# A four-part graph network on one core: the first gathering in two short-float passes, heavy blocks found from the edge list, the root product first, 16 basis sums inside the counting

## What is computed

```python
def rgcn_gate_layer(x, row, col, edge_type, basis, att, gate_w, root, bias):
    w = jnp.einsum('rb,bio->rio', att, basis)          # 2 x 512 x 512 out of 30 bases
    x_j = x[col]
    for r in range(2):
        gate = jax.nn.sigmoid(x_j @ gate_w[r, :, 0])
        msgs.append(gate[:, None] * x_j @ w[r])
    msg = jnp.where((edge_type == 0)[:, None], msgs[0], msgs[1])
    agg = jax.ops.segment_sum(msg, row, num_segments=x.shape[0])
    return agg + x @ root + bias
h = relu(rgcn_gate_layer(x, row, col, edge_type, basis1, ...))
out = rgcn_gate_layer(h, row, col, edge_type, basis2, ...)
```

## Time and profile before

| | us |
|---|---|
| median of 3 runs (lowest, highest) | 1159.91 (1156.43, 1161.30) |
| the profiled execution | 1161.15 |
| its span | 1159.4 |

### The profile page before, as it was taken

How to read it: one execution, slowest core, us unless ns; L and a number is a source line. 1 busy time by engine, 2 the same in 40 slices (tenths; PEclk the granted TensorE clock), 3 DMA queues, 4 the chain that set the end, 5 groups by cost and what they waited for, 6 DMA issues and landing times. The chain is left out here.

```text
span 1159.4 us, 15448 instructions
## 1 busy us (share of the span) xinstructions
PE 1086.1 (94%) x4410; PEld 607.0 (52%) x4442; DVE 835.8 (72%) x1852; ACT 558.3 (48%) x978; POOL 559.3 (48%) x518
## 2 busy tenths in 40 slices
PE   3989888899999989899999999999999999999997
PEld 1564222344557453655565565555555557446664
DVE  5694677769755153688788788788888867849997
ACT  0221321310332221477777777777777744116663
POOL 1960112233433330667876666666666300027774
PEclk9988989999999999899999999999999999999999
DMA  7995997657211005595554454445454010026665
GB/s 283 341 404 212 360 400 264 231 184 233 84 48 46 13 14 194 132 259 111 114 110 92 101 98 95 100 95 97 98 98 88 1 55 23 9 93 197 203 206 173
DMA packets 60182, 172.66 MB, mean 149 GB/s; under 512 B 12645, under 2 KB 13189, under 8 KB 52552
## 3 DMA queue, kind: packets, MB, share of 16 engines
q0 software_dynamic: 31536, 72.01, 26.6%
q1 hardware_dynamic: 28568, 99.66, 23.4%
HBM read 159.65 MB, written 11.98 MB: 148 GB/s over the span
## 5 line engine op out<-in xcount | busy, mean ns | idle before, releaser
L1664 PE MATMUL PS<-wide,hidT 128*128 128x512 f32 x672 | 302.1, 592 | 2.2 <-DVE hidT L1540 0.4
L705 POOL DMA_INDIRECT rec_scratch<-rec_src,slot_row x84 | 102.5, 1220 | 252.8 <-DMA rec_scratch<-rec_src,slot_row 208.2
L1664 PEld LDWEIGHTS PS<-wide,hidT 128*128 128x128 f32 x672 | 128.6, 191 | 122.8 <-issue 120.5
L1482 POOL DMA_INDIRECT pair_sum<-table_j,counts_rec x84 | 136.7, 1627 | 27.3 <-issue 25.3
L1598 ACT ACTIVATE wide<-PS 128x512 f32<-128x512 f32 x168 | 100.5, 598 | 99.6 <-PE PS L1648 63.5
L1801 POOL DMA_INDIRECT u_space<-table_j,wide x87 | 86.1, 990 | 108.7 <-DMA table_j<-agg_space 81.8
L1474 POOL DMA_INDIRECT pair_sum<-table_i,counts_rec x84 | 89.5, 1066 | 98.9 <-PE PS L1648 59.5
L1603 ACT ACTIVATE wide<-wide,two 128x512 f32<-128x512 f32 x168 | 120.9, 720 | 6.2 <-DVE wide L1533 6.2
L1533 DVE SCALAR_TENSOR_TENSOR wide<-wide 128x512 f32<-128x512 f32 x168 | 116.4, 693 | 5.8
L1491 POOL DMA_INDIRECT rec_scratch<-rec_src,slot_row x84 | 89.5, 1066 | 40.9 <-issue 21.6
L1608 ACT ACTIVATE wide<-wide 128x512 f32<-128x512 f32 x168 | 105.8, 630 | 5.3
(11 more groups left out here) (325 smaller groups left out, 1884.9 us busy)
## 6 DMA issues: line engine op xcount, KB each, us to landing
pieces<-basis_rows SPq DMA_DIRECT2D x56, 1024.0 KB, 7.5
ring<-basis_low SPq DMA_DIRECT2D x30, 256.0 KB, 6.4
w_scratch<-pieces SPq DMA_DIRECT2D x112, 32.0 KB
counts_rec<-rec_scratch SPq DMA_DIRECT2D x1, 2856.0 KB, 9.8
rec_scratch<-rec_src,slot_row POOLq DMA_INDIRECT x168, 2.3
root<-L_gnn_root SPq DMA_DIRECT2D x2, 1024.0 KB, 8.0
rows_in<-in_rows_in SPq DMA_DIRECT2D x2, 1024.0 KB, 13.9
w_rel<-w_scratch SPq DMA_DIRECT2D x1, 2048.0 KB, 11.6
```

Source lines behind the costliest of these rows:

```text
L705: nc.gpsimd.indirect_dma_start(out=rec3_dram, out_offset=bass.IndirectOffsetOnAxis(ap=slot_row[:, 1, t:t + 1], axis=0), in_=rec, in_offset ...
L1482: nc.gpsimd.indirect_dma_start(out=pair_sum[:, t % GOT3, :], out_offset=None, in_=tables[0][1], in_offset=bass.IndirectOffsetOnAxis(ap=idx ...
L1664: m = nc.tensor.matmul(o, hidT[:, t % 2, k * P:(k + 1) * P], w2[:, k, :], start=False, stop=(k == KT - 1), skip_group_check=True)
```

## The change

- **Heavy blocks from the edge list.** `largest`, `mark_heavy` and `heavy` go. Instead VectorE copies the group masks in the sort (`both_kinds` at e = 10), TensorE sums edges per pair of source and target chunk in seven products (`pair_sums`, e = 20), VectorE and TensorE reduce them (`sums_of_groups` at e = 44, `block_sums` at e = 50, `sums_of_blocks` at e = 74), and `heavy_blocks(0)` and `heavy_blocks(1)` follow at e = 74, each six steps longer than before. A block with 4095 or more edges in all counts as heavy.
- **First gathering in short float.** Its ten rows stand in ten slots of their own in `pieces` (`first_rows`); ScalarE rounds them (`first_high`, into the space of `packed`, so behind the last unpacking) and rounds the counts (`counts_rounded`) between the last products, VectorE takes the rests (`first_low`). The two splits of count blocks stand ahead of this, right behind the last unpacking. TensorE takes the first term of all chunks, then waits for all parts, adds the rests and takes the 95 other passes.
- **Order of layer 2.** The five root products stand ahead of the gates and products. SP's program is as before.
- **Basis sums.** 16 of 60 stand in the counting, one behind the one-hots of each tile from 62 to 77; 4, 6, 6, 6, 6 ahead of the chunks' adds, 16 behind them.
- **Records** are set at e = 40 of the sort.
- TensorE loads four block numbers to registers right behind the counting and two more ahead of the second gathering.

```diff
-            rests = pieces_short[:, 4 * NT, :].rearrange("p (j n) -> p j n", j=4)
+            first_hi = nc.alloc_sbuf_tensor_at("first_hi", [P, 2 * NT, D], F32R, offset=packed_at)
+            rests = nc.alloc_sbuf_tensor_at("rests", [P, 4, P], F32R, offset=packed_at + 8 * NT * D)
...
+            FIRST_SLOT = 4 * (RING1 - 1)
+            first_rows = pieces[:, FIRST_SLOT:FIRST_SLOT + 2 * NT, :]
+            first_lo = pieces_short[:, FIRST_SLOT:FIRST_SLOT + 2 * NT, :]
+            first_at = lambda r, c: (2 * c + r + KT) % (2 * NT)
...
-            SUM2_BEFORE_H1 = (16, 11, 11, 11, 11)
+            SUM2_COUNT = range(62, 78)
+            SUM2_BEFORE_H1 = (4, 6, 6, 6, 6)
+            PAIR_SUMS_AT, BLOCK_SUMS_AT = 20, 50
...
+                FIRST_TERMS = [(m_, r, part) for m_ in range(NT) for r in range(2) for part in (first_hi, first_lo)]
+                def gathered_first(c, terms):
+                    for m_, r, part in terms:
+                        pe.wait_ge(sem("counts_short"), 2 * m_ + r + 1)
+                        pe.wait_ge(sem("first_lo" if part is first_lo else "first_hi"), 2 * m_ + r + 1)
+                        m = nc.tensor.matmul(PS[:, c, :], counts_short[r][:, m_, c * P:(c + 1) * P], part[:, first_at(r, m_), :],
...
+                def pair_sums():
+                    pe.wait_ge(sem("src_group"), 3)
+                    for g in range(ET // SUM_TILES):
...
+                pe.wait_ge(sem("heavy_at"), 2)
+                rest_chunk = [rest_numbers(j, 8, NT - 1) for j in range(2)]
+                rest_first = [rest_numbers(j, 12, 2 * NT - 1) for j in range(2)]
                 early_late = Y0_LATE[0]
...
-                for c in range(NT):
-                    gathered_first(c)
+                pe.wait_ge(sem("rests"), 2)
+                for c in range(NT):
+                    gathered_first(c, FIRST_TERMS[:1])
+                pe.wait_ge(sem("first_hi"), 2 * NT)
+                pe.wait_ge(sem("first_lo"), 2 * NT)
+                for j in range(2):
+                    rest(rests[:, j, :], rest_chunk[j], (first_hi, first_lo), rest_first[j])
+                for c in range(NT):
+                    gathered_first(c, FIRST_TERMS[1:]).then_inc(sem("o0_mm"), 1)
                     if c:
                         pe.wait_ge(sem("h1"), c)
                         turn_rows(c - 1, turn(("T1", c - 1), alone))
 
                 for c in range(NT):
-                    if c == 1:
-                        pe.wait_ge(sem("h1"), NT)
-                        turn_rows(NT - 1, turn(("T1", NT - 1), alone))
-                    pe.wait_ge(sem("side_ev"), side["T1", c] + 1)
+                    if c == 0:
+                        pe.wait_ge(sem("root_in"), 32)
+                        for d in range(NT):
+                            if d == 1:
+                                pe.wait_ge(sem("h1"), NT)
+                                turn_rows(NT - 1, turn(("T1", NT - 1), alone))
+                            pe.wait_ge(sem("side_ev"), side["T1", d] + 1)
+                            root_rows(d)
                     gates(1, (c,), turn(("G1", c), alone))
...
-                    if c in HEAVY_AT:
-                        heavy(HEAVY_AT.index(c))
-                pe.wait_ge(sem("root_in"), 32)
-                for c in range(NT):
-                    root_rows(c)
...
                 for j in range(2):
-                    rest(rests[:, j, :], rest_numbers(j, 8, NT - 1), (y_hi, y_lo), rest_numbers(j, 4, 2 * NT - 1))
+                    rest(rests[:, j, :], rest_chunk[j], (y_hi, y_lo), rest_numbers(j, 4, 2 * NT - 1))
...
+                    if e == 10:
+                        both_kinds()
+                    if e == 40:
+                        records()
+                    if e == 44:
+                        sums_of_groups()
+                    if e == 74:
+                        sums_of_blocks()
+                        heavy_blocks(0)
+                        heavy_blocks(1)
...
                 for t in range(NS):
                     count_hots(t)
-                    if t == 6:
-                        records()
+                    if t in SUM2_COUNT:
...
+                        sum2(SUM2_COUNT.index(t))
...
                 for c in range(NT):
                     unpack(2, c)
+                split_block(0)
+                split_block(1)
+                for n in range(2 * NT):
+                    first_low(n)
...
-                done = 0
+                done = len(SUM2_COUNT)
...
+                def first_high(n):
+                    r, c = Y0[n]
+                    at = first_at(r, c)
+                    act.wait_ge(sem("counts"), 3 * NT)
+                    act.wait_ge(sem("side_ev"), side["Y0", r, c] + 1)
+                    nc.scalar.copy(first_hi[:, at, :], first_rows[:, at, :]).then_inc(sem("first_hi"), 1)
+                def counts_rounded(m, r):
+                    act.wait_ge(sem("rests"), 2)
+                    nc.scalar.copy(counts_short[r][:, m, :], counts[r][:, m, :]).then_inc(sem("counts_short"), 1)
...
                     for m in LATE_MIX[n]:
                         keep_stage(piece(m), m)
+                    if n == FIRST_HIGH_AT:
+                        for i in range(n + 1):
+                            first_high(i)
+                    if n > FIRST_HIGH_AT:
+                        first_high(n)
+                        for _ in range(ROUNDED_PER[n]):
+                            counts_rounded(*rounded.pop(0))
...
-                for r in range(2):
-                    for m in range(NT):
-                        act.wait_ge(sem("rests"), 2)
-                        nc.scalar.copy(counts_short[r][:, m, :], counts[r][:, m, :]).then_inc(sem("counts_short"), 1)
```

More of the change, by code:

```diff
@@ L1189, in _ @@
+                    for j in range(2):
+                        b = dve.value_load(heavy_at[0:1, 16 + j:17 + j], min_val=0, max_val=NT * NT - 1)
+                        block = blocks[1][:, bass.ds(b, 1), :].rearrange("p b n -> p (b n)")
+                        nc.vector.tensor_tensor(block, block, rests[:, j, :].bitcast(F32), ALU.add).then_inc(sem("all_edges"), 1)
+                        dve.wait_ge(sem("all_edges"), 2 + NT + j)
                 for c in range(NT):
@@ L1209, in _ @@
                 low_parts(2 * NT - 1)
-                heavy_blocks(1)
                 dve.wait_ge(sem("deg"), 1)
@@ L1357, in _ @@
                         nc.scalar.copy(y_hi[:, NT * r + c, :], y_rows[:, NT * r + c, :]).then_inc(sem("y_hi"), 1)
-                    if c in HEAVY_AT:
-                        g = HEAVY_AT.index(c)
-                        keep_product(("heavy", g), found_of[g], rows=slice(0, 1))
-                for r in range(2):
-                    for m in range(NT):
-                        act.wait_ge(sem("rests"), 2)
-                        nc.scalar.copy(counts_short[r][:, m, :], counts[r][:, m, :]).then_inc(sem("counts_short"), 1)
                 act.wait_ge(sem("deg"), 1)
```

251 lines of the change are left out of this document (150 added, 101 removed).

## The result

| | before | after |
|---|---|---|
| median of 4 runs, us (lowest, highest) | 1160.61 (1156.43, 1162.22) | 1178.99 (1177.73, 1179.57) |
| the profiled execution's span | 1159.4 | 1177.2 |
| granted clock, mean | 0.985 | 0.970 |

What follows compares the result with a forecast made beforehand. TensorE was taken as the bound, mostly also in sort and counting. Terms 2 + 5.4 + 0.8 + 0.6 + 3.0 + 2.5 = +14.3 us gave 1175.5 profiled, 1174 as median; range 1158 to 1183.

Steps and rivals of the forecast that it cites:

- sort: In the sort, added copies and small sums on VectorE and extra passes on TensorE cost +2 us (0 to 3).
- 16 sums in the counting: In tiles 64 to 71, eight basis sums on VectorE delay the one-hot of tile 72 by 5.4 us (3 to 7).
- register loads behind the counting: Behind the counting, four register loads on TensorE, partly run ahead during the last mix, cost +0.8 us (0 to 2.7).
- gathering and root wait: At the first gathering, 18.7 us saved on TensorE vanish waiting for the root matrix; the root product starts +0.6 us later.
- tail of layer 2: Ahead of the second gathering, an uncovered scale, round and subtract plus register loads, net +3.0 us (2 to 4).
- clock, outside the counting: Slow clock behind the 14 us root wait and longer counting waits: +2.5 us in all (0 to 5).
- near 28: Listed sign that the forecast is right: the first gathering itself takes near 28 us instead of 44.8.
- The third of three is the same case: On SP's queue, root as third 1 MB load lands 11.4 us after the first load's issue, at 285.4.
- Rival (c): At SP's queue, faster low rows let root2 land early, at 276; time 1152 to 1154 us, chance 0.10.
- Rival (b): In sort and counting, insertions mostly hidden, one-hots running six tiles ahead; root wait stays: 1163 us (1158 to 1166), chance 0.17.
- a later wait for basis rows takes some: In the sort, a later TensorE wait for basis rows absorbs part of 2.6 us of added work, leaving +2.
- Partly run ahead: Behind the counting, some of the four register loads' 2.0 us overlaps the last mix, leaving +0.8.

Runs made afterwards that it cites:

- later-by-nine-tiles kernel: The kernel before with only the 16 basis sums put in the counting, behind the one-hots of tiles 71 to 86 instead of 62 to 77: ratio 1.0029.

## Why the prediction was right, and where its sizes were off

The prediction held in direction and in its main step; the terms against what was measured:

| term | forecast | measured |
|---|---|---|
| sort | +2 | -0.4 |
| 16 sums in the counting | +5.4 | +5.9 |
| register loads behind the counting | +0.8 | +2.7 (2.51 idle) |
| gathering and root wait | +0.6 | +0.0 |
| tail of layer 2 | +3.0 | +2.9 |
| clock, outside the counting | +2.5 (all of it) | +7.7 |
| rest | | -0.2 |
| sum | +14.3 | +18.6 |

**Gathering and root wait.** Right step by step. The working gave 30.5 us for the gathering (240.04 to 270.5) and 29.9 were measured; the "near 28" in the prediction's list of signs doesn't follow from it. Counted from the first gathering's start: sum 17 at +12.1 was carried over from before, it came at +11.5 (261.24); root2's issue was put at +35.0 and came at +34.0; its landing at +45.4 and came at +44.8. Chunk 0's turn was to wait 3 us and waited 2.83. "The third of three is the same case" gave the value, and the reordering of the queue showed that this was so: 5.9 us for root as the first, 10.8 as the third. The landings kept the order of issue in both. By the rule of the Trainium skill (page "DMA: Bandwidth & Descriptors", section "Queues, rings and completion order") that completion is not first in, first out, root could have passed the other two; in these traces it did not, in either order. Rival (c), root2 early because the low rows come early, fell on the same rows: they still came behind the loads of w_scratch. Only with the loads put ahead of the stores did what it describes happen.

**The counting.** Right in place and size: eight sums ahead of the one-hot of tile 72 were put at 5.4 us, and from the first unpacking to tile 72 every kernel with them took 5.3 more. The later-by-nine-tiles kernel is what shows the reason. Rival (b), that the ring of six hides them, fell with it. That the first to last count came out at +5.9 is 5.3, less 0.2 ahead of it, plus 0.8 of slow start behind it. One reading was off without a price that shows: the low rows were to be there in time, but the first sum waited 1.28 us for its own at 163.17.

**Tail.** 2.3 bare plus 1.0 of register loads less 0.3 was the sum; the trace has 2.91 + 0.16. The last low part, VectorE's row 355.47 + 0.69, was ready at 356.16, and the first rest began at 356.97. So of the 2.91 us some 2.1 are the tail, and 0.8 lie behind it, where the program has the first register load; the 0.16 stands where it has the second. Both parts were right in kind and near in size.

**Sort: wrong.** Nothing of +2 is to be seen, and one execution could not have shown it. In the nine profiled kernels whose code is the same up to there, the first count came at 102.5 to 106.8; in the three with the old sort at 105.2 to 106.8. In 24 to 106 TensorE waited 4.4 us for basis rows (2.8 before), 4.2 for VectorE's one-hots (5.1) and none for GpSimd's (2.4): the waits changed places, and in all they are 10.9 us where they were 12.2. The step that failed is "a later wait for basis rows takes some": the waits took all of the added work. Which of them gave way to which part of it was not tried.

**Register loads: mis-sized.** "Partly run ahead" was the wrong half. TensorE had nothing queued ahead of them, with the last count just done, so the loads were bare: 2.51 us for four, 0.63 each, where the 1.00 for two gives 2.0; the row of 411.57 came behind two rests, so it need not hold the whole price. The Trainium skill, page "DMA: Bandwidth & Descriptors", section "Latency and other measured facts", gives a `tensor_load` a floor of some 600 ns; an estimate from that figure for four is 2.4 us, and the 2.51 of this trace agrees.

**Clock: mis-sized, the largest error.** The term was taken from one short stretch, 1.7 us lost in 4, for two places. There were three places with a price of their own, by products of one form at either level: 5.22 us for 3.70 behind the register loads, 6.57 for 3.60 behind the wait for root, 15.35 for 13.79 behind the tail's wait; together 6.05. What failed is the step from waits to clock: only the root wait and those in the counting were given a slow start, and the waits of 2.5 and 2.9 us, which the forecast had in its own sum, were not. In the counting, where the clock was to cost, it added little. The granted clock was 0.69 in 178 to 189, and the product at 182.94 took 6.01 us where 3.65 is its time at full clock; but TensorE still waited for VectorE at 192.55 and 193.83, so this was hidden. Only what ran slowly behind tile 72 cost, 0.8 us. The last 1.6 us are chance: the product of 24 records at 429.53 took 7.23 us (5.61 before), and over all twelve profiled kernels, with the same code and nearly the same waits ahead of it (1.35 to 1.48 us, then 0.97 to 1.06), it took 5.6 in six and 6.5 to 7.3 in the other six.

**How much is luck.** The sum was 14.3 for 18.6 in the profiles. Two errors offset each other in part: the sort's +2 that did not come, and 7.1 us too little for register loads and clock. The 1.6 us of chance would have gone another way in half of the executions.

**Moved records.** Worth nothing, as said: the scatters now ran from 82.8 to 414.7 (110.2 to 435.8) and the block's end went the other way.

## What to carry to other kernels

When a stage on the bound engine is shortened, list what the next instruction waits for and when each becomes ready if the stage took no time at all; here two chains (low rows to the 60th sum, low rows to the root load) came ready 10 and 15 us behind the shorter stage, so the transfers had to be moved before the gain could appear. A wait put on TensorE costs its length and a slow start, so cover even 2 or 3 us of it with a product that has no hurry. Work added to another engine should go where that engine is idle, by the trace: eight of the 16 sums stood among the unpackings and cost 5.3 us there; nine tiles on, the profile shows 0.4 us and the timed runs 0.8 to 5.8.

## What the runs showed of the hardware that was not expected

**The price of a slow start does not grow with the wait.** The first eight records of the root product took 6.57 us behind 14.90 us of wait, 6.40 behind 13.28, 6.21 behind 13.11, 6.62 behind 6.19, and 3.60 with no wait. Behind the 9.20 us ahead of the products of layer 2, 16 records took 8.67 for 7.11. The 60 short passes of the second gathering took 15.06 to 15.82 us in the six kernels with 2.90 or 2.91 us of wait ahead of the rests, and 13.77 or 13.79 in the six without. Shorter waits are not certain to cost: behind the register loads (2.50 to 2.68 us) the product of 3.70 took 5.19 to 5.39 in four kernels and 3.69 in the fifth. The Trainium skill (page "TensorE: Matmul & The Clock Gate", section "HAM oscillation — how this bites in real kernels") has each long wait for a transfer pay its slow start anew; for waits of 6 us and more every trace here agrees.

**A load of a block number to a register** costs TensorE's queue 0.63 to 0.67 us when nothing is queued ahead of it (2.50 to 2.68 us for four, in five kernels). Between products it showed no idle time: 32.9 us from the last count to the first gathering, as before the loads were there.
